# Value projection in units of 128 tokens by 512 weight columns, taken in quads, with the value weights' sums on POOL and their low parts on DVE

## The reference

```python
q = (hidden_q @ Wq).reshape(b, lq, h, dh)
k = (hidden_kv @ Wk).reshape(b, lk, h, dh)
v = (hidden_kv @ Wv).reshape(b, lk, h, dh)
score = jnp.einsum('bqhd,bkhd->bhqk', q, k) * scale + position_bias
...
x = x + jnp.tanh(g_xattn[0]) * _L0_xattn_ref(_layernorm(x, axis=-1), ctx_4096, mask_BxSxS2_bk0, fside_Bx32xSxS2_0, L0_xattn_Wq, L0_xattn_Wk, L0_xattn_Wv, L0_xattn_Wo)
x = x + jnp.tanh(g_ffn[0]) * _L0_ffn_ref(_layernorm(x, axis=-1), L0_ffn_c1_w, L0_ffn_c2_w, L0_ffn_w1, L0_ffn_w2t)
```

## Time and profile before

| | us |
|---|---|
| median of 3 runs (1855.85 to 1857.11) | 1856.61 |
| span of the profiled execution | 1854.3 |
| between the span and the median | 2.3 |
| PE busy in the profiled execution | 1840.5 |
| projections, from 0 to | 945 |

### The profile page before, as it was taken

How to read it: one execution, slowest core, us unless ns; L and a number is a source line. 1 busy time by engine, 2 the same in 40 slices (tenths; PEclk the granted TensorE clock), 3 DMA queues, 4 the chain that set the end, 5 groups by cost and what they waited for, 6 DMA issues and landing times.

```text
span 1854.3 us, 37953 instructions
## 1 busy us (share of the span) xinstructions
PE 1840.5 (99%) x15324; PEld 1587.8 (86%) x15324; DVE 1074.6 (58%) x1754; ACT 695.5 (38%) x1773; POOL 957.8 (52%) x758
## 2 busy tenths in 40 slices
PE   9999999999999999999999999999999999999999
PEld 8899988899998888888878888878888888888887
DVE  5443466433345455333447676786766886777663
ACT  4333243322223333333346555555555522222221
POOL 5767688666668888778735333343343121111110
PEclk9999999999999999999999999999999999999999
DMA  5555566644455555457658878798787650000000
GB/s 182 195 175 175 185 193 210 204 159 144 155 175 185 193 185 173 170 199 248 231 201 347 350 270 331 306 368 335 277 323 303 243 209 24 23 28 25 23 12 17
DMA packets 129693, 359.51 MB, mean 194 GB/s; under 512 B 12016, under 2 KB 53360, under 8 KB 118512
## 3 DMA queue, kind: packets, MB, share of 16 engines
q1 hardware_dynamic: 129520, 357.09, 53.7%
HBM read 229.11 MB, written 127.93 MB: 193 GB/s over the span
## 4 chain that ended last, share of the span: by engine, by line
PE 96%; DVE 2%; DMA 1%; POOL 1%; ACT 1%; issue 0%; SPq 0%; DVEq 0%; ACTq 0%
PE bank L1471 28%; PE bank L1473 28%; PE bank L1472 28%; PE bank L1574 4%; PE bank L1538 3%; PE bank L1554 2%; PE bank L1695 1%; PE bank L1672 1%; POOL wv_s_lo L732 0%; DMA ln_x<-in_x 0%; PE bank L1651 0%; DMA raw_tokens_first<-in_ctx_t 0%; PE bank L1638 0%; POOL wkq_lo L732 0%; ACT wv_s_hi L837 0%
## 5 line engine op out<-in xcount | busy, mean ns | idle before, releaser
L1471 PE MATMUL bank<-tokens_hi,wkq_hi 128*128 128x512 f32 x888 | 346.8, 391 | 1.2 <-DVE u L1089 1.0
L732 POOL TENSOR_TENSOR wkq_lo<-raw_wkq,wkq_hi 128x768 fp32r<-128x768 f32 x126 | 283.4, 2271 | 122.0 <-ACT wkq_hi L837 121.8
L1473 PE MATMUL bank<-tokens_hi,wkq_lo 128*128 128x512 f32 x888 | 345.6, 389 | 0.0
L1472 PE MATMUL bank<-tokens_lo,wkq_hi 128*128 128x512 f32 x888 | 345.6, 389 | 0.0
L1471 PE MATMUL bank<-wv_s_hi,tokens_hi 128*128 128x256 f32 x896 | 254.4, 284 | 0.7 <-POOL wv_s_lo L732 0.7
L1473 PE MATMUL bank<-wv_s_hi,tokens_lo 128*128 128x256 f32 x896 | 253.5, 283 | 0.0
L1472 PE MATMUL bank<-wv_s_lo,tokens_hi 128*128 128x256 f32 x896 | 253.5, 283 | 0.0
L1471 PE MATMUL bank<-wo_hi,attn_t_hi 128*128 128x512 f32 x512 | 205.7, 402 | 1.2 <-DVE attn_t_lo L1251 1.2
L1473 PE MATMUL bank<-wo_hi,attn_t_lo 128*128 128x512 f32 x512 | 199.9, 390 | 1.4 <-issue 1.4
L1472 PE MATMUL bank<-wo_lo,attn_t_hi 128*128 128x512 f32 x512 | 199.3, 389 | 0.5 <-issue 0.5
L1471 PEld LDWEIGHTS bank<-tokens_hi,wkq_hi 128*128 128x128 f32 x888 | 166.7, 188 | 36.3 <-DVE u L1089 1.4
(11 more groups left out here) (150 smaller groups left out, 3697.3 us busy)
## 6 DMA issues: line engine op xcount, KB each, us to landing
k_t<-c SPq DMA_DIRECT2D x128, 256.0 KB, 2.4
v_by_token<-c SPq DMA_DIRECT2D x128, 256.0 KB, 2.3
q_t<-c SPq DMA_DIRECT2D x128, 256.0 KB, 2.4
kt<-k_t SPq DMA_DIRECT2D x16, 2048.0 KB, 9.5
qt<-q_t SPq DMA_DIRECT2D x16, 2048.0 KB, 13.8
v<-v_by_token SPq DMA_DIRECT2D x16, 2048.0 KB, 12.4
raw_wkq<-in_wk SPq DMA_DIRECT2D x32, 512.0 KB, 4.1
raw_wv<-in_wv SPq DMA_DIRECT2D x16, 1024.0 KB, 5.9
```

The costliest lines, as they stand in the source:

```text
L732: pool.tensor_tensor(lo, job_raw(r)[:, a:b, :], hi.bitcast(F32), ALU.subtract)\
L1471: pe.matmul(o, a[0], b[0], start=first_mm, stop=False, skip_group_check=not grouped)
L1472: pe.matmul(o, a[0], b[1], start=False, stop=False, skip_group_check=not grouped)
L1473: return pe.matmul(o, a[1], b[0], start=False, stop=last_mm, skip_group_check=not grouped)
```

## The change

A value unit now has 128 tokens as the stationary side and 512 weight columns as the moving side: 42 matmuls of 512 columns, as a key unit has. Four such units (a quad) cover the 512 tokens for one set of 512 weight columns, and use two weight jobs at once. In each half the value units come as four quads with two key units between them, at units 4, 10, 16, 22 and 35, 41, 47, 53. The split value weights of a half have one buffer instead of two. Value blocks are stored in rows of 2 KB instead of 1 KB.

POOL makes the sums of all value jobs, those of a quad's two jobs while the quad before it is on PE; DVE makes their low parts in the two units before the quad, after `u3` and before `c22`. The jobs of the first quad are loaded before unit 0, and the sums of its first job stand in POOL's program before those of key job 2. The raw buffers of key weights get a place of their own, and the raw tokens of set 0 another. Set 1 starts at unit 26 and set 2 at unit 57, and each half of a set takes three units instead of five: its load stands at the start of the unit in which its first chunk is rounded.

```diff
-UNITS = ([("k", 0, u) for u in range(6)] + [("v", 0, u) for u in range(16)] +
...
+def with_quads(half, first):
+    out, u = [("k", half, k) for k in range(first)], first
+    for quad in range(4):
+        out += [("v", half, QUAD * quad + t) for t in range(QUAD)]
+        more = 2 if quad < 3 else 16 - u
+        out += [("k", half, k) for k in range(u, u + more)]
+        u += more
+    return out
+UNITS = (with_quads(0, 4) + with_quads(1, 3) +
...
+def job_at(r):
+    f, is_v, i = JOBS[r]
+    if not is_v:
+        if any(UNITS[f - k][0] == "v" for k in (1, 2)):
+            return f - 4, f - 4, f - 3, f - 3
+        return f - 2, f - 2, f - 1, f - 1
+    if i < 2:
+        return -1, i - 1, f - 2, f - 1
+    if i == 8:
+        return f - 3, f - 2, f - 2, f - 1
+    if i == 9:
+        return f - 6, f - 3, f - 2, f - 1
+    return f - 5, f - 4 + i % 2, f - 2, f - 1
...
-SET_FROM = {1: 22, 2: 52, 3: 64}
+SET_FROM = {1: V_END[0], 2: V_END[1], 3: 64}
+SET_STEPS = 3
...
-                    if n == n0 + 4:
+                    if n == n0 + SET_STEPS:
                         sp.wait_ge(dve_xlo, token_part(i, 0, 2))
                         load_tokens(i, 1)
...
+            sums(V_JOB[0])
             for n in range(NU):
...
-                    sub, k = divmod(n - n0, 5)
-                    if 0 <= sub < 2 and k < 3:
+                    sub, k = divmod(n - n0, SET_STEPS)
+                    if 0 <= sub < 2:
                         token_hi(i, sub, k)
...
+            def weight_lo(r, part):
+                dve.wait_ge(*hi_part_done(r, part))
+                a, b = ((1, 4), (4, 8))[part]
+                hi, lo = (t[:, a - 1:b - 1, :, :] for t in job_dest(r))
+                dve.tensor_tensor(lo, job_raw(r)[:, a:b, :].rearrange("p a (c w) -> p a c w", c=2),
+                                  hi.bitcast(F32), ALU.subtract).then_inc(dve_wlo, 1)
...
                 sum_u3(n)
                 token_step(n, 1)
+                for r, part in LO_DVE:
+                    if job_at(r)[2 + part] == n:
+                        weight_lo(r, part)
...
                 if kind == "v":
-                    for t in range(2):
-                        cols = slice((2 * (u % 2) + t) * P, (2 * (u % 2) + t + 1) * P)
-                        for c in range(2):
-                            mm = three(o[:, t * 256:(t + 1) * 256], hi_lo(tokens, full, XI[m], c, cols),
-                                       hi_lo(weights, full, WI[m], c, full),
-                                       first_of_bank and t == 0 and c == 0, c == 1, False)
+                    cols = slice(u % QUAD * P, (u % QUAD + 1) * P)
+                    for c in range(2):
+                        mm = three(o[:, :], hi_lo(tokens, full, XI[m], c, cols), hi_lo(weights, full, WI[m], c, full),
+                                   first_of_bank and c == 0, c == 1, False)
```

More of the change, by code:

```diff
@@ L35 @@
 KQ_UNITS = [n for n, u in enumerate(UNITS) if u[0] != "v"]
-V_UNITS = [n for n, u in enumerate(UNITS) if u[0] == "v" and u[2] % 2 == 0]
+V_UNITS = [n for n, u in enumerate(UNITS) if u[0] == "v" and u[2] % QUAD == 0 for _ in range(2)]
+V_END = [max(n for n, u in enumerate(UNITS) if u[:2] == ("v", half)) + 1 for half in range(2)]
 JOBS = sorted([(n, False, i) for i, n in enumerate(KQ_UNITS)] + [(n, True, i) for i, n in enumerate(V_UNITS)])
-JOB_OF = {f: r for r, (f, _, _) in enumerate(JOBS)}
-BY_DVE = [JOB_OF[V_UNITS[0]], JOB_OF[V_UNITS[8]]]
+KQ_JOB = {f: r for r, (f, is_v, _) in enumerate(JOBS) if not is_v}
+V_JOB = [r for r, (_, is_v, _) in enumerate(JOBS) if is_v]
+def job_at(r):
[11 more added lines that the diff above has]
+    return f - 5, f - 4 + i % 2, f - 2, f - 1
+BY_POOL = sorted(range(2, len(JOBS)), key=lambda r: (job_at(r)[1], r))
+V_EARLY = [(r, 0) for r in V_JOB[2:]]
+HI_ORDER = [(0, 0), (1, 0), (0, 1), (1, 1)] + sorted(
+    ((r, part) for r in range(2, len(JOBS)) for part in range(2)), key=lambda q: (job_at(q[0])[2 + q[1]], q not in V_EARLY, q))
+LO_DVE = [(r, part) for r, part in HI_ORDER if r in V_JOB]
+LO_POOL = [q for q in HI_ORDER if q not in LO_DVE]
 XI = {1: 0, 2: 1, 3: 2, 4: 6, 5: 3, 6: 4, 7: 5}
@@ L203, in build @@
         lnxo = at("ln_xn_t", [P, CH, P], F32, 204)
-        mask_in = [at(f"mask_in{i}", [P, PPH, 2, S], U8, (206, 205)[i]) for i in range(HALVES)]
+        mask_in = [at(f"mask_in{i}", [P, PPH, 2, S], U8, (160, 205)[i]) for i in range(HALVES)]
         mask_rows = at("mask_by_row", [P, PAIRS, S], U8, 204)
@@ L772, in _ @@
             lo_part(1, 1)
+            sums(V_JOB[0])
             for n in range(NU):
                 for r in range(2, len(JOBS)):
-                    _, a, b = job_at(r)
-                    if a == n:
-                        lo_part(r, 0)
-                    if b == n:
-                        lo_part(r, 1)
+                    for part in range(2):
+                        if job_at(r)[2 + part] == n and (r, part) in LO_POOL:
+                            lo_part(r, part)
                 t, late = divmod(n - LN_AT, 2)
@@ L782, in _ @@
                     do_rstd(t)
-                for r in range(2, len(JOBS)):
-                    if job_at(r)[0] == n and r not in BY_DVE:
+                for r in BY_POOL:
+                    if job_at(r)[1] == n:
                         sums(r)
@@ L911, in _ @@
             for n in range(NU):
+                for r in V_JOB:
+                    if job_at(r)[2] == n and JOBS[r][2] >= 2:
+                        hi_part(r, 0)
                 if n >= 2:
@@ L914, in _ @@
                 for i, n0 in SET_FROM.items():
-                    sub, k = divmod(n - n0, 5)
-                    if 0 <= sub < 2 and k < 3:
+                    sub, k = divmod(n - n0, SET_STEPS)
+                    if 0 <= sub < 2:
                         token_hi(i, sub, k)
                 for r in range(2, len(JOBS)):
-                    _, a, b = job_at(r)
-                    if a == n:
-                        hi_part(r, 0)
-                    if b == n:
-                        hi_part(r, 1)
+                    for part in range(2):
+                        if job_at(r)[2 + part] == n and not (r in V_JOB[2:] and part == 0):
+                            hi_part(r, part)
                 if n == NU - 1:
@@ L1480, in product @@
                 i = SET_OF[kind, half]
-                job = JOB_OF[n] if n in JOB_OF else JOB_OF[n - 1]
+                if kind == "v":
+                    half_jobs = V_JOB[8 * half + 2 * (u // QUAD):8 * half + 2 * (u // QUAD) + 2]
+                    parts_of = half_jobs if u % QUAD == 0 else []
+                else:
+                    parts_of = [KQ_JOB[n]]
                 o = bank[{1: n % 2, 2: n % 2, 6: 2, 7: 3 + n % 2, 4: 3 + n % 2, 5: 5 + n % 2, 3: 5 + n % 2}[m]]
                 first_of_bank = m in (1, 5, 6, 7)
-                tokens, weights = xs[i % 2], job_dest(job)
+                tokens, weights = xs[i % 2], vw[half] if kind == "v" else kw[KQ_UNITS.index(n) % 2]
                 if n == PLAIN:
@@ L1489, in product @@
                 if m == 1:
-                    pe.wait_ge(pool_wlo, weight_part(job, 0))
+                    for r in parts_of:
+                        pe.wait_ge(*lo_part_done(r, 0))
                     pe.wait_ge(act_c11, n - 1)
@@ L1494, in product @@
                 if m == 6:
-                    pe.wait_ge(pool_wlo, weight_part(job, 1))
+                    for r in parts_of:
+                        pe.wait_ge(*lo_part_done(r, 1))
                     if n == PLAIN:
@@ L1787, in blocks, with value_blocks @@
             .reshape(units, P, 4 * 2 * width)
+    def value_blocks(w):
+        w = w.reshape(2, 2, P, G // 2, 2, 2, 256)
+        order = [(1, 0), (0, 0), (0, 1), (1, 1)]
+        return np.stack([w[k, :, :, :, i, :, :].transpose(2, 3, 1, 0, 4) for i, k in order], axis=3)\
+            .reshape(G, P, 4 * 2 * 256)
     gates = np.concatenate([np.broadcast_to(a["g_xattn"].reshape(1, 1), (P, 1)),
```

133 lines of the change are left out of this document (66 added, 67 removed).

## The result

| | before | changed |
|---|---|---|
| median of 4 runs each, us | 1856.86 (1855.85 to 1857.3) | 1879.93 (1878.0 to 1881.1) |
| span of the profiled execution | 1854.3 | 1878.4 |

The ratio is 1.0127, 95% interval 1.0112 to 1.0141: slower by about 23 us, where 12.5 was forecast. The direction is right, the size is not: the loss is nearly twice the forecast one, and the time stands at the upper end of the range.

What follows compares the result with a forecast made beforehand. PE was taken as the bound, busy 1840.5 of 1854.3 us. New waits of 32.1 us less 19.6 removed gave 12.5 more: 1869 us, with a range from 1848 to 1880 and 1862 to 1876 as the forecast's own.

Steps and rivals of the forecast that it cites:

- The gain: In the projections, 32 value units go from 10.08 to 9.52 us by wider matmuls: 17.9 us less.
- The start: Units 2 and 3: PE waits for low parts and `c22` behind POOL's and DVE's sums, 13.3 us; bounds 0 and 15.
- The prediction's own test on the trace before: At the start, DVE's 10.9 us and POOL's 3.0 from 15.79 sum to 29.7, beside 28.93 in the trace.
- The wait for `c22`: Product 3 of unit 2: `c22` comes at 54.8 behind DVE's value lows, wanted at 50.5, so 4.3 us.
- The quads: Quads at 41, 47 and 53: `c22` about 0.5 us late behind two value lows, 1.5 us in all.
- The first quad of the second half: Unit 34's first low part late by 3.3 us and its `c22` by 3.6: 6.9 us, from 3 to 9.
- The token sets: Late key low parts behind token loads and rounding: 5.4 us at unit 30, 2.5 each at 61 and 68; 10.4.
- The rival on the clock: Waits of 7.5, 5.4 and 4.3 us could each lower TensorE's clock, losing 2 us: 1873 to 1875; chance 0.22.
- Sharing between POOL and DVE: On the SBUF port, POOL or a two-SBUF-input DVE operation locks out the other: end near 1869, without it near 1855.
- The rival by which the two run side by side: POOL and DVE do not exclude each other, unit 2 is on time: 1855 us, no change; chance 0.12.
- the weights stay ahead: No POOL or DVE term reaches PE, only the token sets' 10.4 us is left: 1847.4 us, faster; chance 0.22.

Runs made afterwards that it cites:

- e8: The changed kernel with each value matmul cut back into two of 256 columns, in the new order: 1895.19 us, ratio 1.0214 to the kernel before.
- e4: The changed kernel with POOL's sums of the first two value jobs behind key job 2's sums and low parts, key job 3 loaded in unit 0: 1872.07 us.
- e6: The changed kernel with `c22` on DVE ahead of both value low parts where they are first parts, ahead of the second where second parts: 1870.85 us.
- e9: The kernel before, with PE made to wait ahead of six units for chains of 2 to 18 small ACT copies: 1884.22 us, ratio 1.0157.
- e1: The changed kernel with small 128 column matmuls on PE ahead of six of its waits, no wait taken away: 1873.62 us, ratio 1.0098 to before.
- e11: The wide value units with the mended orders together, sums of value jobs 0 and 8 on POOL instead of DVE: 1852.31 us, ratio 0.9983 to before.

## Why the prediction was wrong in size

**The gain (17.9 us)** was right: 0.55 us for each value unit in e8.

**The start (13.3 us)** measured 15.6. Unit 2 began at 36.6 instead of 39.9, and its wait was 3.9, not 7.5. The sum had added every DVE operation in full. All twelve of POOL's sums did meet one, but ten of them grew by 0.32 to 0.47 us beside a subtraction of 0.65 us, and the two beside a low part of 1.13 us by 0.83 and 0.87. The prediction's own test on the trace before had come out 0.8 us too long (29.7 for 28.93). The wait for `c22` was 4.65 (forecast 4.3). Two falls of the clock, 5.0 us together, filled the difference. e4 and e6 show both causes: POOL's order and DVE's order.

**The quads (1.5 us)** measured 1.8, gone in e6.

**The first quad of the second half (6.9 gross)** measured 6.6, with 1.6 of it half clock. The waits there were 2.6 and 1.8 for 3.3 and 3.6, so that the right total is in part luck. (In the sum, 33.7 and a low part of 2.2 make 35.9, not 36.2.) The kernel before has 1.8 in the same units.

**The token sets (10.4 us)** are the term that failed: 20.1 in the table, 20.0 net of before. The waits alone were 6.1, 2.6 and 3.7 where 5.4, 2.5 and 2.5 were forecast, 2.0 less. The other 7.8 are 5.9 of half clock behind these three and 1.9 of small waits and edges. At unit 68 the load landed 7.7 us after its issue, not 6.6.

**The step that failed** is that the sum priced a wait at its length. The rival on the clock had been set aside with "No wait in this trace is long enough to show it", and it priced three falls at 2 us each. There were six, at 1.5 to 2.9 us and some 12 us together, since waits of 2.6 us were long enough too. All waits together were shorter than forecast (28.3 for 32.1), so that the two errors partly cancel. e9 shows that price on the kernel before, and e1 what it comes to on the path: 5.4 us net, because at the start and in unit 34 a faster PE only waits longer, and at unit 68 the load came later.

The table's excess of the changed kernel adds up to 45.4 us: 28.3 of waits, some 12 of half clock, and 5 of edges and small delays behind the waits, for which the sum had nothing. Since e1 gave back only 5.4 us, about half of the 10.6 us missed is the half clock. Beside the sum, e1's columns still have 2.7 us more at unit 68, where the load landed late, 2.4 more in units 33 to 36 and 1.2 in units 8 to 27, where the sum took the quads as hidden.

**Sharing between POOL and DVE** was right as a mechanism, and e4 and e11 show it; its price at the start was set too high. The rival by which the two run side by side is out. So is "the weights stay ahead", whose time of 1847 could only be had by other orders.
